# Second products of 128 columns, evicted by two engines; tile one's norm and transposes inside the first recurrence

## What is computed

```python
xn = layernorm(x)
xp = silu(xn @ W_in.T)
alpha = sigmoid(xp @ W_alpha.T + b_alpha); beta = sigmoid(xp @ W_beta.T + b_beta)
v = tanh(xp @ W_v.T + b_v)
h_t = alpha_t * h_{t-1} + beta_t * v_t           # scan over the 4096 tokens
x1 = x + (h * silu(h)) @ W_out.T
y = layernorm(x1)
h1 = rmsnorm(y)
q = h1 @ Wq + bq;  k, v = split(((h1 @ Wdown + bdown) @ Wup + bup))
att = softmax(q k^T / 8) over the 16 heads g of one token   # btd,btgd->bthg
u = y + (att v) @ Wo + bo
gate = softmax(rmsnorm(u) @ Wg + bg)             # 8 experts
out = x1 + u + sum_e gate_e * (rmsnorm(u) @ We[e])
```

## Time and profile before

| | us |
|---|---|
| median of 3 runs | 2241.36 (2018.11 to 2354.70) |
| profiled execution | 2015.93 |
| its span (slowest core, the one shown) | 2014.3 |
| spans of the 8 cores | 2005.1 to 2014.3 |
| TensorE busy | 1896.7 (94%) |
| VectorE busy | 1267.4 (63%) |
| ScalarE busy | 739.4 (37%) |
| POOL busy | 211.6 (11%) |

### The profile page before, as it was taken

How to read it: one execution, slowest core, us unless ns; L and a number is a source line. 1 busy time by engine, 2 the same in 40 slices (tenths; PEclk the granted TensorE clock), 3 DMA queues, 4 the chain that set the end, 5 groups by cost and what they waited for, 6 DMA issues and landing times.

```text
span 2014.3 us, 32221 instructions; the slowest of 8 cores (2005.1 to 2014.3 us)
## 1 busy us (share of the span) xinstructions
PE 1896.7 (94%) x11008; PEld 900.6 (45%) x11008; DVE 1267.4 (63%) x2146; ACT 739.4 (37%) x1971; POOL 211.6 (11%) x208
## 2 busy tenths in 40 slices
PE   4787667999999999999999999999999999999899
PEld 2343333444444444454444544444444544444444
DVE  2745657865478646776468755786467764676544
ACT  3343634431435333533325334343335424352200
POOL 3621120210001100020001200021000200011000
PEclk9888868999999999999999999999999999999999
DMA  8995373657534283335642375333843364423343
GB/s 266 341 324 137 69 136 65 175 149 223 196 126 147 105 257 140 147 127 157 220 168 108 126 204 204 114 142 123 249 150 133 126 179 158 145 105 126 126 149 144
DMA packets 72909, 326.48 MB, mean 162 GB/s; under 512 B 31136, under 2 KB 31136, under 8 KB 39712
## 3 DMA queue, kind: packets, MB, share of 16 engines
q1 hardware_dynamic: 67520, 277.75, 40.8%
q0 software_dynamic: 5232, 46.68, 9.2%
HBM read 303.97 MB, written 48.23 MB: 175 GB/s over the span
## 4 chain that ended last, share of the span: by engine, by line
PE 88%; DVE 4%; issue 3%; DMA 2%; ACT 2%; POOL 1%; DVEq 0%; SPq 0%; ACTq 0%; POOLq 0%
PE bank L369 43%; PE bank L429 14%; PE bank L456 6%; PE bank L604 5%; PE bank L506 5%; PE bank L411 5%; PE bank L542 2%; DMA we<-wall 2%; PE bank L585 2%; PE bank L574 1%; PE bank L527 1%; PE bank L477 1%; DVE F L919 1%; PE bank L571 1%; PE bank L490 1%
## 5 line engine op out<-in xcount | busy, mean ns | idle before, releaser
L369 PE MATMUL bank<-we,h2T 128*128 128x512 bf16 x4096 | 938.5, 380 | 7.6 <-DVE gat L1105 6.5
L887 DVE SCALAR_TENSOR_TENSOR xs<-bank,gat,xs 128x512 f32<-128x512 f32 x512 | 384.1, 750 | 393.9 <-PE bank L369 393.0
L369 PEld LDWEIGHTS bank<-we,h2T 128*128 128x128 bf16 x4096 | 386.4, 98 | 432.8 <-issue 18.5
L297 POOL TENSOR_TENSOR F<-F,sml 128x512 bf16<-128x512 bf16 x128 | 132.9, 1038 | 1445.7 <-DVE sml L1014 1445.7
L429 PE MATMUL bank<-F,wm 128*128 128x512 bf16 x1280 | 280.2, 381 | 4.8 <-POOL wm L285 4.0
L795 ACT ACTIVATE F<-bank,sml 128x128 bf16<-128x128 f32 x512 | 182.0, 371 | 220.0 <-DVE sml L1006 220.0
L429 PEld LDWEIGHTS bank<-F,wm 128*128 128x128 bf16 x1280 | 125.7, 98 | 158.2 <-issue 9.1
L927 DVE SCALAR_TENSOR_TENSOR R<-R 128x512 f32<-128x512 f32 x64 | 46.0, 718 | 102.1 <-ACT R L721 102.0
L815 ACT ACTIVATE tm<-R,sml 128x1024 bf16<-128x1024 f32 x32 | 36.9, 1152 | 193.7 <-DVE R L1065 193.7
L795 ACT ACTIVATION_READ_ACCUMULATOR F<-bank,sml 128x1 f32 x512 | 107.2, 209 | 0.0
L715 ACT ACTIVATE R<-bank,cpfs 128x512 f32<-128x512 f32 x64 | 44.0, 688 | 163.0 <-DVE F L919 115.6
(11 more groups left out here) (118 smaller groups left out, 1852.5 us busy)
## 6 DMA issues: line engine op xcount, KB each, us to landing
we<-wscr SPq DMA_DIRECT2D x128, 1024.0 KB, 5.9
wm<-wscr SPq DMA_DIRECT2D x84, 1024.0 KB, 5.0
wscr<-wall POOLq DMA_DIRECT2D x16, 1024.0 KB, 10.2
out<-xs SPq DMA_DIRECT2D x32, 512.0 KB, 5.1
xs<-wall POOLq DMA_DIRECT2D x14, 1024.0 KB, 9.3
we<-wall POOLq DMA_DIRECT2D x14, 1024.0 KB, 12.1
xs<-x SPq DMA_DIRECT2D x7, 2048.0 KB, 9.0
wscr<-wm SPq DMA_DIRECT2D x6, 1024.0 KB, 18.2
```

Source lines behind the costliest of these rows:

```text
L297: gp.tensor_tensor(pb[j % 3][:, :].rearrange("p (g n) -> p g n", n=128), pb[j % 3][:, :].rearrange("p (g n) -> p g n", n=128), sml[:, RS + ...
L369: mm = pe.matmul(b[:, :], hT[:, kc * 512 + tb * 128:kc * 512 + (tb + 1) * 128], we[ui % NE][:, kc * 512:(kc + 1) * 512], start=(kc == 0), ...
L887: v.scalar_tensor_tensor(dst, bk[6 + k % 2][:, :], gat[(t - 1) % 2][:, tb * 8 + e:tb * 8 + e + 1], dst, OP.mult, OP.add).then_inc(v_ec, 1)
```

## The change

Seven edits, in the words of the code (t counts from 0):

1. Second products: four of 128 columns per step instead of eight of 64. Each multiplies the whole 128 x 128 block, of which half (the pairs that belong together) is used; the result has 512 columns in the bank. Two halves of it are evicted by DVE (`opair`, `orow`, r = 0) and two by ACT (`oev`, r = 1), each of 64 partitions x 128 elements. ACT's come two steps later in its program; TensorE waits for both (`v_o`, `a_o`).
2. Tile 1's x is loaded on the arrival of the third quarter of tile 0's x. DVE takes its statistics before tile 0's recurrence, ACT computes the root after the fifth eviction of `win(0)` and applies it after `win(0)` and in the first chunk of `abv(0)`; TensorE transposes after the groups ci = 8 and 14, in banks 6 and 7, and `win(1)` uses these banks.
3. In `abv(1)` the second half of `t2(0)` stands after ci = 20 instead of 17 and `wdn(0)` after 23 instead of 20; DVE's copies come after the chunks 4 and 6 instead of 5 and 6.
4. In tile 0's attention `wout(1, j)` stands after the transposes of step j instead of before them, and `x1ev` one step later, behind `rsum`.
5. The third norm of tile 0 goes block by block (`ln3_first`, `nb3_first`), into F1.
6. DVE's `xu(0)` now stands behind the last `nb3_first`.
7. In the last tile `xu` is split by block and stands among the expert evictions (`ec`) before `t3`.

The diff, cut to its core:

```diff
+    def opair(j, hl, r):
+        return bk[4 + j % 2][64 * r:64 * r + 64, :].rearrange(
+            "p (k r l u i) -> p k r l u i", k=2, r=2, l=2, i=8)[:, :, r, hl]
...
-        sync.wait_ge(c_cm, 2)
+        sync.wait_ge(s_xb[2], 16)
         load_x(1)
...
-        def t1(t):
-            for p in range(4):
+        def t1(t, parts):
+            for p in parts:
                 if p == 0:
                     pe.wait_ge(a_l1a, t * 4 + 4)
-                    if t == 1:
-                        pe.wait_ge(a_abv, 21)
-                if p == 3 and t == 1:
-                    pe.wait_ge(a_abv, 22)
+                if t == 1 and p >= 2:
+                    pe.wait_ge(v_t1, 3 + p)
+                bb = bkb[6 + p % 2 if t == 1 else p]
...
-                    mm = pe.matmul(bk[4 + mc % 2][:, :],
+                    mm = pe.matmul(bk[(6 if t == 1 else 4) + mc % 2][:, :],
...
+                if t == 0:
+                    if ci == 8:
+                        t1(1, (0, 1))
+                    if ci == 14:
+                        t1(1, (2, 3))
                 if t == 1:
                     if ci == 14:
                         t2(0, (0, 1))
-                    if ci == 17:
+                    if ci == 20:
                         t2(0, (2, 3))
-                    if ci == 20:
+                    if ci == 23:
                         wdn(0)
...
                 if t >= 1:
                     ec(t, 1)
-                elif j < 8:
-                    wout(1, j)
...
                 mm.then_inc(p_ptv, 1)
                 if t >= 1:
                     ec(t, 1)
+                elif j < 8:
+                    wout(1, j)
                 pe.wait_ge(v_ptv, t * 16 + j + 1)
                 if j >= 2:
                     pe.wait_ge(v_o, t * 16 + j - 1)
+                    pe.wait_ge(a_o, t * 16 + j - 1)
                 bo = bk[4 + j % 2]
                 for g in range(4):
-                    for hl in range(2):
-                        mm = pe.matmul(bo[64 * hl:64 * hl + 64, g * 64:(g + 1) * 64],
-                                       ptv[j % 2][:, 512 + g * 64:512 + (g + 1) * 64],
-                                       ptv[j % 2][:, g * 128 + hl * 64:g * 128 + (hl + 1) * 64],
-                                       start=True, stop=True)
+                    mm = pe.matmul(bo[:, g * 128:(g + 1) * 128],
+                                   ptv[j % 2][:, 512 + (g // 2) * 128:512 + (g // 2 + 1) * 128],
+                                   ptv[j % 2][:, g * 128:(g + 1) * 128], start=True, stop=True)
...
         abv(0)
-        t1(1)
         win(1)
...
         def win(t):
             for mc in range(NCH):
                 s.wait_ge(p_win, t * 8 + mc + 1)
...
+                if t == 0 and mc == 4:
                     load_set(SET_LNE)
                     ln1_rstd(1)
                     load_set(SET_SILU)
+            if t == 0:
+                ln1_app(1, 0)
+                ln1_app(1, 1)
+
+        def abv(t):
+            for mc in range(NCH + 1):
+                if t == 0 and mc == 1:
+                    ln1_app(1, 2)
+                    ln1_app(1, 3)
...
+        def oev(t, j):
+            s.wait_ge(p_o, t * 16 + j + 1)
+            for hl in range(2):
+                o = s.activation(out=orow(t, j, hl, 1), in_=opair(j, hl, 1), func=AF.Copy)
+            o.then_inc(a_o, 1)
...
                 r.then_inc(a_p, 1)
+                if j >= 2:
+                    oev(t, j - 2)
...
+        def ln3_first():
+            n2 = N2[0]
+            for b in range(NB + 1):
+                if b < NB:
+                    s.wait_ge(v_u, 2 * b + 2)
...
+                    s.activation(out=sml[:, RU + b:RU + b + 1], in_=sml[:, L3 + b:L3 + b + 1], func=AF.Exp,
+                                 scale=-0.5).then_inc(a_r3, 1)
+                if b >= 1:
+                    s.wait_ge(v_nb3, b)
+                    s.activation(out=F1[:, (b - 1) * D:b * D], in_=ub[:, (b - 1) * D:b * D], func=AF.Identity,
...
                 if mc >= 1:
                     gmul(t, mc - 1)
-                if t == 0:
-                    if 1 <= mc <= 4:
-                        ln1_bn(1, 2 * mc - 2)
-                        ln1_bn(1, 2 * mc - 1)
...
-                if t == 1 and mc in (5, 6):
-                    t2(0, range(4 * (mc - 5), 4 * (mc - 4)))
+                if t == 0 and mc in (2, 4):
+                    t1(1, range(mc - 2, mc))
+                if t == 1 and mc in (4, 6):
+                    t2(0, range(2 * mc - 8, 2 * mc - 4))
...
                 ec(t, 1)
-                if t == 0 and j < 8:
-                    x1ev(1, j)
                 if j + 1 < 16:
                     rsum(t, j + 1)
+                if t == 0 and 1 <= j <= 8:
+                    x1ev(1, j - 1)
...
-                v.tensor_copy(ov, bk[4 + j % 2][:, 0:256].rearrange("p (g u i) -> p g u i", u=8, i=8)
-                              ).then_inc(v_o, 1)
+                for hl in range(2):
+                    o = v.tensor_copy(orow(t, j, hl, 0), opair(j, hl, 0))
+                o.then_inc(v_o, 1)
...
+                if t == 0 and u in (2, 4, 6):
+                    nb3_first(u // 2 - 1)
...
-        t1(0)
+        t1(0, range(4))
+        for u in range(8):
+            ln1_bn(1, u)
+        ln1_aggr(1)
+        ln1_nm(1)
         v.wait_ge(g_set, 1)
         abv(0)
-        t1(1)
...
         wo(0)
+        nb3_first(3)
         v.drain()
         xu(0)
-        nb3(0)
         t3(0)
...
-            ec(t, A_T3 - 2)
+            if t == NT - 1:
+                for b in range(NB):
+                    ec(t, 1)
+                    xu(t, (b,))
+                ec(t, A_T3 - 2 - NB)
+            else:
+                ec(t, A_T3 - 2)
             t3(t)
...
-            xu(t)
+            if t < NT - 1:
+                xu(t)
```

74 lines of the change are left out of this document (41 added, 33 removed).

## The result

| | before | after |
|---|---|---|
| runs, us | 2018.1 lowest | 1969.4 lowest, 1970.8 median |
| profiled execution, slowest core | 2014.3 (core 3) | 1969.9 (core 0) |
| mean span of the 8 cores | 2010.6 | 1966.7 |

The ratio is 0.9761, 95% interval 0.9737 to 0.9784: faster by 2.4%. In some runs of either kernel one half of the chip ran at a lower clock (before up to 2354.7 us, after once 2094.9); ratio and interval leave these out. The forecast was 1966.

What follows compares the result with a forecast made beforehand. TensorE's own work was taken to bound the kernel from 340 us on, leaving the prologue, the last tile's gap and TensorE's work to change. 2015.9 - 10 - 16 - 13 - 4 - 7 = 1966 us, range 1946 to 1990.

Steps and rivals of the forecast that it cites:

- Second products: All tiles, 128 groups: four products of 128 columns take as long as eight of 64; 0 gained, bounds -15 and +10 us.
- First recurrence: Tile one's normalisation and transposes move inside the recurrence; input product one starts at 103.4, 10 us gained (bounds 0 and 15).
- Tile zero's transposes in the second recurrence: Between input product one and the q product, waits for DVE and half clock behind them vanish: 16 us gained (bounds 10, 16.5).
- Tile zero's attention: Transposes first, output product covers the wait; eight steps of 3.7 us each: 13 us gained (bounds 3 and 18).
- Rival B: Tile zero's attention stays at 1.2 GHz, a step 5.1 us: gain 3 instead of 13, total 1976 us; chance 0.14.
- Third norm: Tile zero's third norm, done block by block, ends at about 324.0 instead of 329.4: 4 us gained.
- last tile: Residual sums between expert evictions cut TensorE's 6.46 us wait for the gates to about 1.4: 7 us gained (bounds 5, 7).
- rival C: Second products: leaving the 64-wide form gains 0.12 us per group, total 1951 us; chance 0.07.
- A: Tile one's x lands 6 us later still, or casts hold the copies: first recurrence's gain lost, total 1976; chance 0.15.
- D: Steady attention: an eviction pair beyond 0.52 us makes DVE the bound of 112 steps; 2036 us at 1.15; chance 0.05.
- E: Whole kernel: little changes, the waits come back as waits on the next engine, 2000 us; chance 0.06.

Runs made afterwards that it cites:

- dma_cast: masks_first with the last 12 of GpSimd's 20 weight halves up to the first recurrence cast by their DMA: 1963.7 to 1964.8 us, ratio 0.9736.
- before_wide: The kernel before with only the wide second products (four of 128 columns), evicted by VectorE in four copies: 2010.3 to 2012.0 us, ratio 0.9949.
- x1_old_gate: The changed kernel, but tile one's x load waits for two casts again, as before the change: 1982.7 us (one execution, on slower cores 2 and 3).
- masks_first: The changed kernel with the load of tile two's x issued behind the two attention masks on SyncE's queue: 1960.4 us (one execution).
- ce_late: The changed kernel with GpSimd's first four expert weight casts held back until the masks have landed: 1958.3 and 1960.7 us.
- wout_first: The changed kernel with tile one's output product and its sum again ahead of transposes and row sums in tile zero's attention: 1982.4 and 1989.1 us.
- narrow4: The changed kernel with four second products of 64 stationary and 128 moving columns per step: 1982.2 and 1991.9 us, ratio 0.9844.
- narrow8: The changed kernel with eight second products of 64 by 64 per step, in the new layout: 1981.3 to 1983.0 us, ratio 0.982.
- wide8: The changed kernel with eight second products of 64 moving columns on all 128 stationary columns: 1968.2 and 1975.4 us, ratio 0.9769.
- all_dve: The changed kernel with all four evictions of a second product on VectorE, none on ScalarE: 1978.2 us (one execution).
- masks_first_2: The same kernel as masks_first, timed again beside dma_cast: 1959.3 to 1960.5 us, ratio 0.9714.

## Why the prediction was right or wrong

**The total** was 1966 against 1970.8. From profile to profile it is a gain of 44.5 us (2015.9 to 1971.4) where 50 was forecast. That is better than its terms were. Two terms that stood at nothing failed: the wait for the masks, which was not in the sum (8 us lost), and the second products (12 us gained). Two gains were put too high. One by one:

**First recurrence, 10 forecast, 5.2 in the mean.** The step that failed is the last one: I worked out when input product one *starts* and booked that as the gain at the output product, as if input product one kept its length of 14.0 us. The start came 11.7 us sooner in the mean, more than forecast; the length grew to 20.5 us, because ScalarE and VectorE lag behind TensorE at the end of the recurrence, so that TensorE runs into input product one and stands 5.2 us there (core 0), and runs slower behind the stall (granted clock 0.76 from 104 to 118). dma_cast takes that wait away almost whole; together with the quicker recurrence it is 10 us. I also read core 3, which in this profile is the last to get there, 127.0 where the mean was 121.4; in before_wide, the same code up to here, core 3 is at 121.9 and the mean at 124.0. Core 3 came to 116.1, a gain of 10.9, and that it agrees with my 10 is luck: on it input product one starts 19.2 us sooner and takes 8.3 longer. With a baseline that moves by 2.6 us, the gain of this stage is 5 to 8 us. The parts on the way were off as well: x took 16.7 us (x1_old_gate: 23.6), not 26.2, so ScalarE never waited for it and the recurrence started at 49.4 on core 0, not 53.7. But the early load delayed the second cast (28.35 on core 0, 20.66 in x1_old_gate). Right were that VectorE under GpSimd's casts sets the pace of the recurrence, and that the copies cost no chunk of their own (7.2 us from release to release with a pair and without). The Trainium skill, "SBUF — State Buffer", section "SBUF: two separate sides", has it that a VectorE instruction with two SBUF inputs and a GpSimd instruction that reads SBUF block each other whole. Scan and multiply, at 3.1 and 2.5 us with casts and 1.28 and 0.67 without, agree.

**Tile zero's transposes in the second recurrence, 16 forecast, 16.5 measured.** Right, at the upper bound: L504 waited 0.45 us (core 0). But the step beyond was missing. I asked what is late next on the engines and not on the queues: **the masks were nowhere in the working**, though moving everything up by 21 us moves the scores towards a DMA whose place depends on SyncE's queue and on the GpSimd casts. In the sum the wait stood at nothing without a reason. 8.2 us of the 21.7 gained were lost there, and masks_first and ce_late give them back with 2 us more. I had asked of the steps that move what they would meet, and not of the DMAs that stand still.

**Tile zero's attention, 13 forecast, 7.5 measured.** The mechanism (the order, and with it the clock) is shown by wout_first, at 13 us. Rival B did not come: the granted clock is 0.99 to 1.00 of full speed from 217 to 245 on core 0, over nearly all of the steps 0 to 7. Mis-sized were the eviction pair (0.61 to the next instruction, I had 0.45) and the latency from copy to eviction (1.38, I had 1.20 from a row at another order), 4.05 instead of 3.7 us over eight steps: 3 us. From the scores to the end of step 8 the stage gained 11.2 us in the mean, where I had 15.1. The rest stands in the last seven steps, where ScalarE sets the pace: a plain one takes 3.38 us, where before it took 2.59, and the seven grew by 3.4 us together on core 0. I had put 1.7. The granted clock is 0.50 in these steps, in both kernels.

**Third norm, 4 forecast, 3.4 measured; last tile, 7 forecast.** The waits of TensorE for gates in the last tile went from 6.46 us to 1.68:

```profile
1855.31 20.02 PE L378 MATMUL bank<-we,h2T 128*128 128x512 bf16 x92 [1.68 <-DVE gat L1150]
```

With the clock that it lost before, that is about 7 us of the 19.5. No run takes the edit of the last tile alone; before_wide, which has the wide products without it, stands at 1669.0 in this stage and the changed kernel at 1660.8, so 8 us are left for it and for what else changed there. Both terms are right as far as that shows.

**Second products, 0 forecast, 12 measured.** The term failed, and rival C (0.12 us a group, chance 0.07) is what happened. The step at fault was the comparison in the earlier trace rows: I measured the group from its own start to the next group's, 0.24 against 0.24, and concluded that no switch is paid. Most of the price stands ahead of the group, where the expert products lasted 1.82 us instead of 1.72, and I had not compared that side. narrow4 and narrow8 bring the price back, wide8 doesn't, before_wide gains it in the other kernel. The Trainium skill, "TensorEngine Tiling (Array Packing)", section Key Properties, says that a change of tiling mode drains the engine. A price at the change agrees with that, 0.09 us on the way in and at most 0.02 on the way out; that it is a drain no run shows. I had written that the trace shows neither of its two rules; a price at the edge was there, in rows that I didn't read. Its other rule, that tiles run in parallel, still finds nothing here: eight products of 64 by 64 take 0.24 us as a group, and eight of 128 by 64 in wide8 take 0.24. (By the 0.12 us that I worked out for that rule the time would have been 1981, not 1980.)

**Rivals.** A did not come, though x1_old_gate shows its mechanism: a late x costs 8 us at the q product. D did not come, and all_dve shows that it needs more than 1.2 us of evictions. E had the right idea, waits on something else that take the place of those removed, at 8 us for the masks and 5 for ScalarE and not at 34 in all; I had not asked the queues.

## A version that beats both

masks_first is the changed kernel with one line moved. In masks_first_2 its median of four is 1960.4, ratio 0.9714 (0.9695 to 0.9733) to the kernel before, where the changed kernel has 0.9761 (0.9737 to 0.9784). The two were timed on different chips; their mean spans, 1954.7 to 1955.5 against 1964.1 to 1966.7, are 10 us apart. What dma_cast gains in the recurrence, 10 us, may be open to whoever brings the masks in sooner as well; that was not tried.

## What to carry to other kernels

When a change moves a whole stretch up, list every DMA that is wanted behind it and ask of each when it is issued and what is ahead of it in its queue and beside it on the DMA engines: a wait that did not exist before has no row in the trace before. When you price an instruction form, measure from the end of its neighbour on each side, and not only the group itself; a price of mode is paid at an edge. Take a gain at the mark where it counts: a stage that starts sooner can take longer. And read a stage on all cores, and in a second profile if there is one, before taking its gain from the slowest core.
